# A four-block transformer kernel: one routing stage reordered, and its start rearranged

## The reference, cut to what matters

```
x = x + L0_xattn(_layernorm(x), ctx)   # self-attention masked to its diagonal, cross-attention, feed-forward
x = x + L0_ffn(_layernorm(x))          # 8 experts, the best one for each token, 128 slots each
x = x + L1_xattn(_layernorm(x), ctx)   # 2 heads
x = x + L1_ffn(_layernorm(x))          # 16 slots attend to the tokens, 16 experts, tokens attend to the slots
x = x + L2_xattn(_layernorm(x), ctx)   # 1 head
x = x + L2_ffn(_layernorm(x))          # 8 experts, the best two for each token, 640 slots each
x = x + L3_xattn(_layernorm(x), ctx)   # 16 heads
x = x + L3_ffn(_layernorm(x))          # 8 experts, the best two, no capacity
```

```
scores = jnp.where(diag[None, :, :], scores, -jnp.inf)
attn = jax.nn.softmax(scores, axis=-1)
sa = jnp.einsum('bnm,bmc->bnc', attn, v) @ sa_out_w.T + sa_out_b
x = _ln(tgt + sa, ln1_g, ln1_b)
```

```
mask = jax.nn.one_hot(jnp.swapaxes(topi, 0, 1), N_EXP, dtype=jnp.int32)
rank = jnp.cumsum(mask.reshape(TOP_K * N, N_EXP), axis=0).reshape(TOP_K, N, N_EXP) - 1
mask = mask * (rank < capacity)
```

## Time and profile before

| what | value |
|---|---|
| time, median of 3 runs | 701.31 us (699.08 to 701.66) |
| the profiled execution: its own time | 694.51 us |
| its span, first to last instruction | 692.7 us |
| busy: PE, PEld | 494.1 us (71%), 379.6 us (55%) |
| busy: DVE, ACT, POOL | 350.3 us (51%), 221.7 us (32%), 264.9 us (38%) |
| chain that ended last, by engine | PE 55%, DVE 18%, POOL 11%, issue 7%, DMA 5% |
| mean granted TensorE clock | 0.795 of full |

### The profile page before, as it was taken

One profiled execution on the slowest core, in us unless ns is written; L12 is line 12 of the kernel. 1 busy time (PEld: TensorE's weight loads), 2 busy tenths in 40 slices (PEclk: granted clock), 3 DMA queues, 4 the chain that ended last, 5 costly groups with the idle time before them and its releaser, 6 DMA issues.

```text
span 692.7 us, 8591 instructions
## 1 busy us (share of the span) xinstructions
PE 494.1 (71%) x3011; PEld 379.6 (55%) x3011; DVE 350.3 (51%) x1109; ACT 221.7 (32%) x426; POOL 264.9 (38%) x376
## 2 busy tenths in 40 slices
PE   1787793646658866697873019999049957999997
PEld 1543473636545452443763019999025356899997
DVE  3869628751188642159876014331286684333333
ACT  1661542203233530051330006442044334344441
POOL 3870757471344201146246760556465051000000
PEclk9999697556955997689555559999659966899999
DMA  8999600001180004860001122211350000000002
GB/s 285 296 147 182 227 1 0 5 25 33 36 281 0 1 0 144 208 196 1 1 0 43 53 60 58 70 57 41 91 161 1 1 0 0 1 1 1 1 1 62
DMA packets 62235, 48.06 MB, mean 69 GB/s; under 512 B 6361, under 2 KB 53493, under 8 KB 62064
## 3 DMA queue, kind: packets, MB, share of 16 engines
q1 hardware_dynamic: 59120, 42.45, 23.7%
q0 software_dynamic: 3072, 5.06, 2.3%
HBM read 35.08 MB, written 13.68 MB: 70 GB/s over the span
## 4 chain that ended last, share of the span: by engine, by line
PE 55%; DVE 18%; POOL 11%; issue 7%; DMA 5%; ACT 3%; SPq 1%; POOLq 0%; DVEq 0%
PE ps L982 9%; PE ps L944 6%; POOL tok L1788 5%; PE ps L882 3%; PE ps L884 3%; PE ps L883 3%; PE ps L592 3%; PE ps L604 3%; DVE rz L1352 3%; DVE st L1265 3%; PE ps L704 2%; POOL rstd L1698 2%; PE ps L647 2%; PE ps L770 2%; PE ps L637 2%
## 5 line engine op out<-in xcount | busy, mean ns | idle before, releaser
L592 PE MATMUL ps<-con,xn 128*128 128x128 f32 x128 | 32.1, 399 | 64.2 <-ACT xn L1157 33.2
L1855 POOL DMA_INDIRECT res<-qT,dest x48 | 47.0, 979 | 65.6 <-DVE qT L1537 55.0
L1563 DVE SCALAR_TENSOR_TENSOR x<-ps,gate,x 128x128 f32<-128x128 f32 x128 | 36.0, 345 | 62.8 <-PE ps L982 62.8
L982 PEld LDWEIGHTS ps<-moe_w,big 128*128 128x128 f32 x512 | 63.2, 196 | 4.1 <-issue 1.7
L592 PEld LDWEIGHTS ps<-con,xn 128*128 128x128 f32 x128 | 21.8, 205 | 77.2 <-DVE xn L1281 66.7
L982 PE MATMUL ps<-moe_w,big 128*128 128x128 f32 x512 | 63.6, 280 | 0.1
L1199 ACT ACTIVATE big<-ps,col 128x512 f32<-128x512 f32 x64 | 44.0, 687 | 58.9 <-PE ps L884 58.5
L1788 POOL DMA_INDIRECT tok<-r,to_slot x48 | 47.2, 984 | 31.5 <-DVE to_slot L1426 17.8
L1707 POOL TENSOR_SCALAR negmean<-mv 128x4 f32<-128x4 f32 x44 | 11.3, 256 | 119.1 <-DVE mv L1268 117.9
L1184 ACT ACTIVATE big<-ps 128x320 f32<-128x320 f32 x64 | 27.1, 439 | 76.8 <-PE ps L884 76.6
L1157 ACT ACTIVATE xn<-x,negmean,rstd 128x128 f32<-128x128 f32 x48 | 21.0, 485 | 91.5 <-POOL negmean L1710 91.5
(11 more groups left out here) (277 smaller groups left out, 1159.3 us busy)
## 6 DMA issues: line engine op xcount, KB each, us to landing
ring<-in_ew SPq DMA_DIRECT2D x21, 256.0 KB, 4.9
moe_w<-in_m0w SPq DMA_DIRECT2D x16, 256.0 KB, 6.5
moe_w<-in_m2w SPq DMA_DIRECT2D x16, 256.0 KB, 5.4
big<-res SPq DMA_DIRECT2D x12, 256.0 KB, 4.7
moe_w<-in_ew SPq DMA_DIRECT2D x11, 256.0 KB, 5.3
tok<-zero SPq DMA_DIRECT2D x1, 2580.0 KB, 31.1
big<-tok SPq DMA_DIRECT2D x8, 322.5 KB, 3.1
ring<-in_ewg SPq DMA_DIRECT2D x9, 256.0 KB, 4.9
```

The source lines that it names most:

```text
L592: last = nc.tensor.transpose(ps[2 * t][:, cols(c)], from_, ident)
L982: last = mm(ps[7 - i % 2][:, cols(c)], big[:, f, i % B, cols(c)], w[:, e, F + P * f:F + P * f + P], start=f == 0, stop=f == FC - 1)
L1563: last = v.scalar_tensor_tensor(out=x[:, C * t + c, :], in0=ps[7 - i % 2][:, cols(c)], scalar=gate[:, C * t + c, e:e + 1], in1=x[:, C * t ...
L1855: g_.indirect_dma_start(out=res_d[name], out_offset=bass.IndirectOffsetOnAxis(ap=dest[:, at:at + 1], axis=0), in_=ysb[:, e % 2, cols(b)], ...
```

## The change

It does four things.

1. SEQ2's tiles stand four stages apart (`SKEW = [1, 1, 4, 1]`; the other lists keep one stage). The semaphore counts, which depended on the distance, are now tallied from the same loop (`nth`).
2. SEQ2 gets a stage `second` after `choose`, which finds the tile's second choices, and four stages `send` at its end, of two indirect transfers each: two for the first choices, two for the second. A tile's first `send` also waits until all earlier sends have landed. `count` counts first choices, second choices and the number of first choices so far. The slot of a second choice is reckoned from the end of the expert's region, so that it no longer needs the first choices of later tiles; which second choices are dropped is found after the wave, for the weights alone.
3. x is loaded first and tile by tile; `con`, the first two squares and `col` are issued by ScalarE; `row` is loaded in two parts. `prepared("L0")`, `neg`, `keys_by_heads` and `round_keys` move into SEQ0 as stages `keys`, `heads` and `round`, and take banks 6 and 7.
4. L0's diagonal self-attention becomes one matmul: `fuse` makes the product of its two weights, plus identity, and its bias, once; `project` by L0v and GpSimd's "so" residual go.

```diff
-SEQ0 = [("stats", None, "x"), ("scale", "xn"), ("turn", "xn", D, None, "so"), ("project", "L0v"), ("out", "L0so"),
-        ("stats", "out", "r"), ("scale", "xn"), ("turn", "xn", D, "1", "mo"), ("project", "L0q"), *attention("L0"),
+SEQ0 = [("stats", None, "x"), ("scale", "xn"), ("fuse",), ("turn", "xn", D, None, None), ("keys",), ("out", "L0so"),
+        ("stats", "out", "r"), ("scale", "xn"), ("turn", "xn", D, "1", "mo"), ("heads",), ("project", "L0q"), ("round",),
+        *attention("L0"),
...
-        ("choose", "m2"), ("count", "m2"), ("place", "m2")]
+        ("choose", "m2"), ("second", "m2"), ("count", "m2"), ("place", "m2"),
+        *[("send", i) for i in range(4)]]
...
+SKEW = [1, 1, 4, 1]
+def in_turn(seq, skew):
+    for step in range(len(seq) + skew * (B - 1)):
+        for t in reversed(range(B)):
+            if 0 <= step - skew * t < len(seq):
+                yield step - skew * t, t
...
-            sp.dma_start(con[:, :], ins["con"]).then_inc(ld_c, 16)
-            sp.dma_start(col[:, :], ins["col"]).then_inc(ld_c, 16)
-            sp.dma_start(sq[:, 0:SQ_AT["L0o"][1]], ins["sq"][:, 0:SQ_AT["L0o"][1]]).then_inc(ld_w, 16)
-            sp.dma_start(row[:, :], ins["row"].to_broadcast([P, ROW_N])).then_inc(ld_r, 16)
+            for t in range(B):
+                sp.dma_start(x[:, C * t:C * t + C, :], ins["x"][t].rearrange("(c p) d -> p c d", p=P)).then_inc(ld_x[t], 16)
+            sp.dma_start(row[:, 0:ROW_1], ins["row"][:, 0:ROW_1].to_broadcast([P, ROW_1])).then_inc(ld_r0, 16)
+            sp.dma_start(sq[:, SQ_AT["L0q"][0]:SQ_AT["L0o"][1]], ins["sq"][:, SQ_AT["L0q"][0]:SQ_AT["L0o"][1]]).then_inc(ld_w, 16)
+            sp.dma_start(row[:, ROW_1:], ins["row"][:, ROW_1:].to_broadcast([P, ROW_N - ROW_1])).then_inc(ld_r, 16)
             sp.dma_start(neg_in, ins["neg"]).then_inc(ld_r, 16)
-            sp.dma_start(x[:, :, :], ins["x"].rearrange("b (c p) d -> p (b c) d", p=P)).then_inc(ld_x, 16)
...
+                    if name == "m2":
+                        up_to(t, ps[2 * t][:, C * E:2 * C * E], B * C)
+                        for c in range(C * t + C):
+                            last = mm(ps[2 * t][:, 2 * C * E:2 * C * E + E], ones[:, :], oh[:, c, :], start=c == 0, stop=c == C * t + C - 1)
...
+            act.dma_start(con[:, :], ins["con"]).then_inc(ld_c, 16)
+            act.dma_start(sq[:, 0:SQ_AT["L0so"][1]], ins["sq"][:, 0:SQ_AT["L0so"][1]]).then_inc(ld_vo, 16)
+            act.dma_start(col[:, :], ins["col"]).then_inc(ld_c, 16)
...
+            def from_the_end(t):
+                kk, two = chunks(t), slice(nb + C * t, nb + C * t + C)
+                count, keep, at = gb[:, two, :], gt[:, kk, :], lg2[:, kk, :]
+                link(v.tensor_copy(first_n[:, :], ps[2 * t][:, 2 * C * E:2 * C * E + E]))
+                link(v.tensor_copy(count, ps[2 * t][:, C * E:2 * C * E].rearrange("p (c e) -> p c e", e=E)))
+                link(v.tensor_tensor(keep, count, bc(first_n[:, :], [P, C, E], [1]), ALU.add))
+                link(v.scalar_tensor_tensor(out=keep, in0=keep, scalar=float(CAP2), in1=oh[:, two, :], op0=ALU.is_le, op1=ALU.mult))
+                link(v.tensor_tensor(at, bc(K("last2"), [P, C, E], [1]), count, ALU.subtract))
+                link(v.tensor_tensor(at, at, keep, ALU.mult))
+                link(v.tensor_reduce(slot[:, two], at, AX.X, ALU.add))
+                v.tensor_scalar(to_slot[:, two], slot[:, two], SKIP, None, ALU.add).then_inc(idx_ready, 1)
...
+            def fuse():
+                def stage(t):
+                    if t == 0:
+                        dve.wait_ge(fuse_mm, 1)
+                        v.tensor_tensor(W("L0v"), ps[7][:, 0:D], ident, ALU.add).then_inc(fused, 1)
+                        dve.wait_ge(ld_r0, 16)
+                        v.tensor_tensor(ROW("so_b"), ROW("so_b"), ps[7][:, D:2 * D], ALU.add).then_inc(fused, 1)
+                return stage
+            def keys():
+                def stage(t):
+                    if t == 0:
+                        dve.wait_ge(ld_r, 32)
+                        prepared("L0")
+                    if t == B - 1:
+                        v.memset(neg[:, :].bitcast(F32), 0.0).then_inc(negs, 1)
+                        dve.wait_ge(negs, 1)
+                        v.tensor_copy(neg[0:16, :], neg_in).then_inc(negs, 1)
...
+            def send_some(i):
+                def stage(t):
+                    if i == 0:
+                        pool.wait_ge(sent, 16 * (B * C + 2 * C * t))
+                    pool.wait_ge(idx_ready, nth("place", 1, t) - (i < 2))
+                    for c in range(C * t + 2 * (i % 2), C * t + 2 * (i % 2) + 2):
+                        send("m2", c + (i >= 2) * B * C)
+                return stage
```

More of the change, by code:

```diff
@@ L105, with tally, nth @@
 TURNS_TO_SLOTS = sum(q[0] == "turn" for q in SEQ0 + SEQ1)
+SKEW = [1, 1, 4, 1]
[4 more added lines that the diff above has]
+                yield step - skew * t, t
 def wavefront(make, seq):
     stages = [make[name](*how) if name in make else None for name, *how in seq]
-    for step in range(len(stages) + B - 1):
-        for t in reversed(range(B)):
-            if 0 <= step - t < len(stages) and stages[step - t]:
-                stages[step - t](t)
+    for i, t in in_turn(seq, SKEW[SEQS.index(seq)]):
+        if stages[i]:
+            stages[i](t)
+SEQS = [SEQ0, SEQ1, SEQ2, SEQ3]
+SIGNALS = {"tokens": lambda q: q[0] == "fsoft" or q[0] == "scale" and q[1] != "x3", "scale": lambda q: q[0] == "scale",
+           "turn": lambda q: q[0] == "turn", "mix": lambda q: q[0] == "mix", "project": lambda q: q[0] == "project",
+           "rounded": lambda q: q[0] == "project" and q[1] != "Dk" and q[1] != "L0v", "maxima": lambda q: q[0] == "maxima",
+           "out": lambda q: q[0] in ("out", "down", "fout"), "fsoft": lambda q: q[0] == "fsoft", "stats": lambda q: q[0] == "stats",
+           "fold": lambda q: bool(q[0] == "turn" and q[4]), "router": lambda q: q[0] == "router", "choice": lambda q: q[0] in ("choose", "second"),
+           "count": lambda q: q[0] == "count", "place": lambda q: 2 * (q[0] == "place" and q[1] == "m2") or q[0] == "place"}
+def tally(signal):
+    out, n, first = {}, 0, 0
+    for seq, skew in zip(SEQS, SKEW):
+        at = [i for i, q in enumerate(seq) if signal(q)]
+        for i, t in in_turn(seq, skew):
+            if i in at:
+                n += int(signal(seq[i]))
+                out[first + at.index(i), t] = n
+        first += len(at)
+    return out
+NTH = {kind: tally(signal) for kind, signal in SIGNALS.items()}
+def nth(kind, k, t):
+    return NTH[kind][k, t]
 SQUARES = [("L0v", 128), ("L0so", 128), ("L0q", 128), ("L0k", 128), ("L0mv", 128), ("L0o", 128),
@@ L299, in build @@
         half = sb("half", [P, C])
+        early = sb("early", [P, 1])
         mx = sb("mx", [P, B * C, 16])
@@ L829, in stage @@
                     last.then_inc(cum_mm, 1)
                 return stage
-            make = dict(turn=turn, project=project, out=out_tokens, up=up, down=down, score=score, maxima=maxima, prob=prob,
+            def fuse():
+                def stage(t):
+                    if t == 0:
+                        pe.wait_ge(ld_vo, 16)
+                        pe.wait_ge(ld_c, 32)
+                        mm(ps[7][:, 0:D], W("L0v"), W("L0so"), start=True, stop=True)
+                        mm(ps[7][:, D:2 * D], V("L0bv").to_broadcast([P, P]), W("L0so"), start=True, stop=True).then_inc(fuse_mm, 1)
+                return stage
@@ L833, in _ @@
+            def keys():
+                def stage(t):
+                    if t == 0:
+                        pe.wait_ge(ld_w, 16)
+                        pe.wait_ge(fused, 2)
+                        prepare("L0", keys_in)
+                return stage
+            make = dict(turn=turn, project=project, fuse=fuse, keys=keys, out=out_tokens, up=up, down=down, score=score, maxima=maxima, prob=prob,
                         mix=mix, fscore=fscore, fsoft=fsoft, fout=fout, router=router, values=values, dscore=dscore, dturn=dturn,
@@ L1159, in scale @@
                 return stage
-            make = dict(stats=stats, scale=scale, turn=turn, project=project, prob=prob, up=up, dscore=dscore, dturn=dturn, score=counted, fscore=counted, fsoft=fsoft)
             def round_keys(name):
@@ L1166, in round_keys, with round_, stage, chances @@
                 A(KR[name][0:a["PD"], :, :], KB[name][0:a["PD"], :, :], ACT.Identity).then_inc(kr_ready, 1)
-            def chances():
-                act.wait_ge(gate_e, n["moe"] + 1)
+            def round_():
+                def stage(t):
+                    if t == 0:
+                        round_keys("L0")
+                return stage
+            make = dict(stats=stats, scale=scale, turn=turn, project=project, prob=prob, up=up, dscore=dscore, dturn=dturn, score=counted, fscore=counted, fsoft=fsoft)
+            make["round"] = round_
+            def chances(ready, count):
+                act.wait_ge(ready, count)
```

(10 more changed lines are left out.)

286 lines of the change are left out of this document (147 added, 139 removed).

## The result

The changed kernel takes 721.41 us (median of 4, 717.55 to 724.12) against 700.19 for the kernel before in the same runs: ratio 1.0318, 95% interval 1.0273 to 1.0362. Two repeats, each with its own runs of before, gave 1.030 (1.0261 to 1.0339) and 1.0253 (1.0221 to 1.0286). It is slower by about 20 us; the forecast was 709, +8, with 688 to 721 as range. The sign and the order of the queues came as forecast, the size did not.

What follows compares the result with a forecast made beforehand. VectorE and hand-overs between engines were taken to bound SEQ2's wave, GpSimd's sends the stretch behind it. Start -6 us and second routing +14 gave +8 on the 701.31 median: 709 us, range 688 to 721.

Steps and rivals of the forecast that it cites:

- The queues: SEQ2's wave: tile 2's second stats precede the first send on GpSimd, first send about 80.6 us in, then sends with gaps.
- It works as meant: Rival, chance 0.17: sends of three tiles vanish behind other tiles' stages; with the start, -20 us, 681.
- the two parts cancel: Rival, chance 0.14: first send at 72 us, start gains 6 to 9; total 698 to 701.
- the coarse sum: Second routing: each step as long as its longest stage, scaled by 0.96; place at 67, first send at 72 us.
- The signs named for being right: First send 78 to 84, last 120 to 128 us into the wave; start's second stats 14 to 15, prob about 41.
- those for being wrong: Signs against the forecast: first send before 73, last before 112, or prob before 37 or after 45 us.
- When tile 0 can send: Second routing: VectorE's 51 us of work plus 10.4 and 14.2 waiting end tile 0's place at 75.6, first send 80.6.
- the walk: Step-by-step reckoning through the engines' queues, giving the first send at 80.6 us and, at the start, the first score at 36.0.
- The clock in the holes: Second routing: VectorE's later waits taken as 14.2 us; TensorE at half clock in them adds some 7, first send 88.
- half clock: Rival, chance 0.2: TensorE stays at 1.2 GHz through the wave; first send 88, last 132, +16 us, 717.
- Until the last send: Second routing, GpSimd bound: 39.7 us of sends, 1.9 of stats, 2.0 of landing waits; last send at 124.2, 14 later.
- The start: Kernel's start: tile 0's second stats at 14.4 us instead of 26.33, prob about 41 instead of 46.83; gain 6, ends 3 and 12.

Runs made afterwards that it cites:

- r_before: The kernel before, unchanged, traced again on the same chip as the repeat of the changed kernel: 694.15 us (one execution).
- r_after: The changed kernel again, nothing altered, on the same chip as the repeated kernel before: 716.43 us, ratio 1.030 to before.
- a_start: The changed kernel with its second routing put back as in the kernel before, so only the start differs: 694.93 us, ratio 0.996 to before.
- a2_heads: Changed start, routing of before, with the heads stage moved right behind keys: 693.56 us, ratio 0.9932 to before; repeated, 694.83 us, 0.994.
- r_before2: The kernel before once more, unchanged, one look on another chip; its own total time is not given.

## Why the prediction was wrong

The forecast was +8 us and about +20 came. Its steps, against the fair pair (r_before, r_after) where the routing is concerned:

- *The queues.* Right in the order of the work. Tile 2's second `stats` stand between `place` and the send (5.4 us from the slots at 375.45 to the send at 380.89, forecast 5.0), then bare sends, with three breaks (two forecast); the last is 133 us after the first `project`. "It works as meant" (681) and "the two parts cancel" fell: at none of the three distances of tiles does the first send come before that of the kernel before, and the coarse sum (72) is off by 15 us. The signs named for being right failed on the late side (first send 78 to 84, last 120 to 128, second `stats` 14 to 15), and those for being wrong had no bound there for the sends.
- *When tile 0 can send.* Right in its form, 5.9 us short: `place` ended at +81.5, forecast 75.6. VectorE's work up to there came at 51.5, forecast 51 (though the terms given for tile 0 add up to 17.9, not to 18.8). Of VectorE's holes, forecast 10.4 + 14.2, came 10.8 until the first reciprocal; 1.09, 1.78 and 1.05 at steps 7, 8 and 12 (forecast 1.0, 1.8, 1.0); 1.61 behind the weight splits (3.2); 2.33, 3.11 and 2.04 behind `out` and `fscore` (1.5, 1.5, 1.9); 4.17 at step 21 (2.3); and two before a reciprocal that I had not seen (1.09 and 0.89). They sum to 30.0, 5.4 more than forecast. 4.4 of it are the two sorts of hole with a chain of TensorE steps in them, and there the walk had taken the full clock: at the full clock the hole behind `fscore` is 1.47, as forecast; for the one at step 21 no run shows the length at the full clock without filler.
- *The clock in the holes.* This is the step that failed: "I take 80.6, since it follows the queues", with "all TensorE work in the waits above at half clock" kept as the upper end. The first send came at 87.0: the term of 14.2 us for the later waits measured 19.2, and 4.4 of these 5.0 us lie in holes with TensorE steps, which it had at the full clock. The rival *half clock* had nearly these times (88 and 132; 87.0 and 133.0), but its condition, 1.2 GHz through the wave, held only in part: the granted clock is 0.50, the 1.2 GHz level, in the 14 us ahead of the first send, but 1.00 from 14 to 28 us, and 0.70 on average, as before the change. So that 88 is so close is partly luck: two holes that nobody had foreseen (2.0 us) stand against the splits' 3.2 that came as 1.6. The row of `router` at 1.71 us and the 0.59 of the tail had pointed to the slow steps. That this level costs the single steps their length is shown; that the first send would come at 80.6 without it is not. With the rule of the Trainium skill (TensorE: Matmul & The Clock Gate, section on HAM oscillation) that bursts between waits fall back to half rate again and again, the trace agrees in the main, with 0.50 to 0.76 in five of the wave's six stretches of 14 us. It does not bear out the prediction's reading of it, nearly every step at 1.2 GHz: the sixth stretch has 1.00.
- *Until the last send.* 46.0 us, forecast 43.6. The term that was mis-sized is the wait for landings: 1.8 us for each tile, not 1.0, as the next send starts 3.05 us after the one before and not at its landing at 2.3. With `stats` in front of the second tile the three breaks are 2.3, 2.1 and 1.8.
- *Behind the last send nothing changes.* Right: 288.6 and 288.8 us.
- *The start.* Forecast 6, came 2.8 (a_start's ratio times 700). The walk held from the second `stats` on: 21.6 us from there to the first `score` forecast, 22.0 measured. What failed is "tile 0's second `stats` starts at 14.4": it started at 18.16. `neg` was not the bound; the first normalization was, four times 2.1 us on GpSimd, which began only at 7.92 behind a copy that waits for `col`, and VectorE's `keys` stands in its queue behind tile 3's `scale`. I had set 14.4 by the transfers' landing alone. a2_heads shows the second half: `heads` at step 9 cost 3.5 us of `prob` (45.66 in a_start, 42.18).
- *The sum.* The fair pair's spans differ by 23.4 us, forecast 8. Start: 0.75 us sooner at the first `project`, forecast 6. From there to the first send: 17.6 us longer, forecast 10.3. Send phase: 6.3 longer, forecast 4.0. Behind it 0.2. So the four were missed by 5.3, 7.3, 2.3 and 0.2, 15 us together. In the medians the change is 21.2 us and the miss 13. The difference of 2 lies in single executions, as a_start's ratio gives 2.8 us for the start and this pair 0.75.

## What to carry to other kernels

When a change spreads a pipeline out, price every TensorE step that stands between two instructions of the bound engine at the clock that the thin stretches show, not at the full one: here that gives the upper end, 88, and 87.0 came. An engine that is to hide work in a wave must be free at the moment the work becomes ready; look first at what its own queue holds there. And follow a gain to the end of the phase: work that is moved from in front of the first send may come back between the sends (7.8 us became 2.5). A start is as early as its slowest chain: a transfer that lands sooner is worth only what the next engine in line can take.

## What the runs showed of the hardware

In some sessions, each on one chip, VectorE's wait for TensorE's last matmul of a burst ends late while GpSimd issues indirect transfers: in r_before2 6.23 and 7.80 us idle where r_before has 0.97 and none. Nine other traces have it (the changed kernel's first and its second repeat, and all of the four kernels of the first set among them). Where it was seen, the list of transfers gives no time to landing for the sends; before, and the changed kernel:
```profile
tok<-r,to_slot POOLq DMA_INDIRECT x48, 2.3
```
```profile
tok<-r,to_slot POOLq DMA_INDIRECT x48
```
The kernel before had medians of 694.03 and 695.20 us in the two later sets without it, and of 697.98, 699.97 and 698.77 in the three with it; whether it makes the difference is not shown. Behind the last send r_before2 takes 2.3 us more than r_before (290.9 and 288.6). What makes it stays open.
